# GpSimd and ScalarE make five of the eight parts of the lanes' one-hots

## The reference

```
h = max(layernorm(x), 0)
x = x + attention_layer(h, src, dst, ...)     # weights: softmax over each node's incoming edges
h = max(layernorm(x), 0)
x = x + message_layer(h, [src, dst], etype)   # 4 steps, each: 4 products by edge type,
                                              # segment_sum over the edges, a GRU cell
# attention: segment_sum(exp(e - max) * Wh[src], dst), e from s_s[src] + s_d[dst]
# messages:  etypes = argmax(edge_attr); a = segment_sum(trans[etypes, src], dst)
```

## Time and profile before

| what | value |
|---|---|
| median of three runs | 416.37 us (415.9 to 416.38) |
| the profiled execution | 417.0 us, its span 415.0 us |
| mean granted clock of TensorE | 0.979 of full speed |
| busy over the span: TensorE, VectorE, ScalarE, GpSimd | 88%, 64%, 36%, 24% |

### The profile page before, as it was taken

One profiled execution on the slowest core, in us unless ns is written; L12 is line 12 of the kernel. 1 busy time (PEld: TensorE's weight loads), 2 busy tenths in 40 slices (PEclk: granted clock), 3 DMA queues, 4 the chain that ended last, 5 costly groups with the idle time before them and its releaser, 6 DMA issues.

```text
span 415.0 us, 6625 instructions
## 1 busy us (share of the span) xinstructions
PE 364.1 (88%) x2057; PEld 246.0 (59%) x2057; DVE 265.3 (64%) x797; ACT 150.9 (36%) x333; POOL 99.8 (24%) x139
## 2 busy tenths in 40 slices
PE   1469798778899979887999999999999999999993
PEld 0458455555677756443756755665846566647792
DVE  6899998999998757774456434455444355344134
ACT  3363577444565354432313121323132131213121
POOL 3100300000000001000777002776005773017300
PEclk9969989999999998999999999999999999999998
DMA  5300000000000000123133202242112332012200
GB/s 136 88 1 2 0 2 2 1 2 1 2 2 2 2 0 0 53 101 109 47 105 103 90 0 88 53 146 58 77 44 66 96 114 86 17 76 56 54 14 24
DMA packets 14499, 19.88 MB, mean 48 GB/s; under 512 B 2592, under 2 KB 7729, under 8 KB 14461
## 3 DMA queue, kind: packets, MB, share of 16 engines
q1 hardware_dynamic: 10276, 12.90, 8.8%
q0 software_dynamic: 2912, 5.97, 5.9%
q10 hardware_dynamic: 1272, 0.54, 0.5%
HBM read 8.27 MB, written 11.13 MB: 47 GB/s over the span
## 4 chain that ended last, share of the span: by engine, by line
PE 65%; DVE 21%; issue 6%; ACT 3%; DVEq 2%; POOL 1%; DMA 0%; SPq 0%; ACTq 0%; POOLq 0%
PE small L1635 29%; PE big L1617 8%; DVE cell_hot L977 7%; PE big L1477 4%; PE small L1514 4%; DVE scores L996 3%; DVEq L977 2%; PE small L1656 2%; PE small L1669 2%; PE big L1580 2%; PE big L1582 1%; PE big L1581 1%; PE small L1580 1%; PE small L1571 1%; PE small L1582 1%
## 5 line engine op out<-in xcount | busy, mean ns | idle before, releaser
L1635 PE MATMUL small<-nibbles,store 128*128 128x384 fp8e4 (+1 forms) x640 | 125.8, 353 | 1.7 <-issue 0.9
L482 POOL DMA_INDIRECT scores<-messages,w_gat x91 | 87.0, 956 | 121.5 <-DMA messages<-store 95.0
L1635 PEld LDWEIGHTS small<-nibbles,store 128*128 128x128 f16 x640 | 62.3, 98 | 64.8 <-issue 7.7
L977 DVE TENSOR_SCALAR cell_hot<-iota,cell_w,fields 128x320 bf16<-128x320 f16 x231 | 64.9, 356 | 1.0 <-issue 0.6
L1477 PE MATMUL big<-cell_hot,store 128*128 128x320 bf16 x231 | 43.2, 324 | 13.9 <-DVE cell_hot L977 11.2
L750 ACT CAST store<-digit_words 128x512 f16<-128x512 f32 x40 | 24.6, 618 | 82.6 <-DVE digit_words L1146 82.6
L1146 DVE TENSOR_TENSOR digit_words<-big,edge_rows 128x512 f32<-128x512 f32 x40 | 27.4, 690 | 41.1 <-PE big L1617 41.1
L1477 PEld LDWEIGHTS big<-cell_hot,store 128*128 x231 | 31.3, 144 | 23.3 <-issue 21.1
L1617 PE MATMUL big<-wT,h 128*128 128x512 f32 x80 | 39.8, 615 | 2.3 <-ACT h L746 2.3
L1089 DVE SCALAR_TENSOR_TENSOR cell_hot<-rz,cell_hot 128x256 f32<-128x256 f32 (+2 forms) x29 | 11.0, 380 | 36.3 <-ACT cell_hot L721 36.3
L468 POOL TENSOR_TENSOR rstd<-var_e,power 128x2 f32<-128x2 f32 x5 | 3.5, 696 | 125.7 <-DVE var_e L1134 125.7
(11 more groups left out here) (262 smaller groups left out, 492.2 us busy)
## 6 DMA issues: line engine op xcount, KB each, us to landing
messages<-store SPq DMA_DIRECT2D x40, 256.0 KB, 2.0
scores<-messages,w_gat POOLq DMA_INDIRECT x91, 2.6
xn<-in_x SPq DMA_DIRECT2D x1, 576.0 KB
out<-xn SPq DMA_DIRECT2D x4, 128.0 KB
store<-in_edge_attr SPq DMA_DIRECT2D x1, 256.0 KB
wn<-in_L_gnn_W_edge SPq DMA_DIRECT2D x1, 256.0 KB, 6.6
wn<-in_L_gnn_Wi ACTq DMA_DIRECT2D x1, 192.0 KB, 4.0
wn<-in_L_gnn_Wh_g ACTq DMA_DIRECT2D x1, 192.0 KB, 6.4
```

The costliest lines, as they stand in the source:

```text
L482: g.indirect_dma_start(out=rows16[:, u].rearrange("p a f -> p (a f)"), out_offset=None, in_=table_rows[s % 2][:], in_offset=bass.IndirectO ...
L977: last = v.tensor_scalar(half_hot[:, (before + q) % RING], iota[:, b * HALF:(b + 1) * HALF], cell_w[:, j % CELL_SETS, bass.ds(tile, 1)], f ...
L1635: last = mm(bank[:, 0:w], m16[s % 2][:, i, t, part], A8[:, t % 2, i, lo:lo + w, t // 2], start=(i == 0 and part == 0 and t == 0), stop=(i ...
```

## The change

VectorE makes only parts 0 to 2 (`LANES_DVE`). For parts 3 to 7 three instructions take the place of the comparison: GpSimd subtracts the column's number from the lane into `lane_gap` (`h1` read as 16-bit numbers) and squares the gap in place; ScalarE then makes max(0, 1 - square), which is 1 where the two agree and 0 elsewhere. There is one `lane_gap`, so the gap of a part waits for the bend of the part before it. The windows wait for the bent parts in place of VectorE's.

```diff
+LANES_DVE = 3
...
+        lane_gap = h1[:].bitcast(F16).rearrange("p (l k) -> p l k", l=P)
...
             norm_scale()
 
+            def lane_gaps(k):
+                done = k - LANES_DVE
+                if k == LANES_DVE:
+                    pool.wait_ge(S0.lanes16, 1)
+                    pool.wait_ge(C.lane_no, 1)
+                else:
+                    pool.wait_ge(S0.bent_lanes, done)
+                g.tensor_tensor(lane_gap, lanes16[:, k * LANE_PART:(k + 1) * LANE_PART].unsqueeze(1)
+                                .to_broadcast([P, P, LANE_PART]), lane_no, ALU.subtract).then_inc(S0.lane_gap, 1)
+                pool.wait_ge(S0.lane_gap, done + 1)
+                g.tensor_tensor(lane_gap, lane_gap, lane_gap, ALU.mult).then_inc(S0.lane_square, 1)
+
+            lane_gaps(3)
+            lane_gaps(4)
             pool.wait_ge(S0.bias_sb, 1)
             pool.wait_ge(E1.sq, 1)
...
+            for k in range(5, LANES_MADE[-1]):
+                lane_gaps(k)
+
             def chunk_scale(y, c):
...
+            def lane_bends(k):
+                act.wait_ge(S0.lane_square, k - LANES_DVE + 1)
+                a.activation(lane_hot[:, :, k * LANE_PART:(k + 1) * LANE_PART], lane_gap, ACT.Relu,
+                             bias=ones[:, 0:1], scale=-1.0).then_inc(S0.bent_lanes, 1)
+
...
                 if J == 1:
+                    lane_bends(4)
                     score_row()
+                if J in (3, 4, 5):
+                    lane_bends(J + 2)
                 if there(J - 3):
                     attn_out(J - 3, J - 3)
...
             for j in range(2, CELL_SETS):
                 window_cells(j)
+            lane_bends(3)
             act.wait_ge(S0.Wh_ps, 2)
...
-                for k in range(LANES_MADE[j - 1] if j else 0, LANES_MADE[j]):
+                for k in range(LANES_MADE[j - 1] if j else 0, min(LANES_DVE, LANES_MADE[j])):
                     lane_hots(k)
...
-                pe.wait_ge(S0.lanes, LANES_MADE[j])
+                pe.wait_ge(S0.lanes, min(LANES_DVE, LANES_MADE[j]))
+                if LANES_MADE[j] > LANES_DVE:
+                    pe.wait_ge(S0.bent_lanes, LANES_MADE[j] - LANES_DVE)
```

More of the change, by code:

```diff
@@ L283, in build @@
         C = sems("c_", "limits iota pads const ident ident16 free lane_no")
-        S0 = sems("s0_", "chain lane_rows lanes_T lanes16 rows ranks ranks_T best best_T table fields_T fields b_diag "
+        S0 = sems("s0_", "chain lane_rows lanes_T lanes16 bent_lanes lane_gap lane_square rows ranks ranks_T best best_T table fields_T fields b_diag "
                   "w_T w_sb bias_sb hn stats var rstd norm lanes "
```

## The result

The changed kernel takes 457.5 us (median of four runs, 456.77 to 458.65), the kernel before on the same chip 416.38 us (415.9 to 416.91). The ratio is 1.1002, with a 95% interval of 1.0975 to 1.1028: slower by 41.1 us. The profiled execution has a span of 455.0 us, 40.0 more than before.

The account below looks back on a forecast made before the run. VectorE, working 109.88 of 115 us while edges are counted, was taken to bound the kernel. 10 x 5.5 - 1.1 - 7.0 = +46.9 us gave 463 us, range 416 to 478 (the forecast case alone 431 to 474).

Parts of the forecast that it names:

- VectorE bounds the stretch; the five parts are worth 7.0 us: Edge counting, 20 to 135 us: VectorE works 109.88 of 115 us; five lane parts at 1.40 us leave it.
- 5.5 us per GpSimd instruction: Each gap or square over 128x2560 elements on GpSimd was taken at 5.5 us, between bounds of 2.25 and 6.6.
- The term of 55 us: Ten GpSimd gaps and squares at 5.5 us each, charged to VectorE as standing still.
- The lower reading of the text: GpSimd's gaps and squares: two reads in turn with the write beside them, 4.4 us each.
- A hold of full length: VectorE stands still for the whole of each GpSimd instruction: 463 us; chance 0.72 together with the variant.
- The lenient reading of the power at 17.07 us: GpSimd holds VectorE only while data pass, 2.25 us per instruction: +14.4 us, 431 us, the forecast's own lower end.
- the variant in which VectorE always gets ahead: GpSimd starts only when VectorE runs out of twelve ring slots; 10 us waiting per part, +43 us; chance 0.72 with the forecast.
- The bends at nothing, the waits of TensorE for bent parts at nothing: ScalarE's five bends, 2.4 us each, fit idle time (12 us without cover); TensorE doesn't wait for gap, square and bend, 13.4 us.
- GpSimd's chain for the edge scale: Behind the second gap and square, it ends at 58.6 us, 14 us later, with VectorE arriving 19.5 us later; costs nothing.
- A slow TensorE keeps pace, so new pauses of 5.5 us cost little beyond themselves.: After pauses, at lower clock, TensorE's window products take 0.28 us each, as VectorE's half one-hots do; costed at nothing.
- The 0.66 of the earlier trace: TensorE's mean granted clock in the ten microseconds after its 4.86 us wait, read as partly 1.2 GHz of 2.4.

Follow-up runs that it names:

- e4: Changed kernel with each GpSimd gap and square cut to 20 of 2560 elements, all waits between engines kept: 409.38 us, ratio 0.9829 to the kernel before.
- e1: Kernel before, all eight lane parts on VectorE, plus ten long two-input GpSimd instructions whose results nobody uses: 458.77 us (+42.6).
- e9: Changed kernel with all eight lane parts made by VectorE again and read from there, GpSimd's ten instructions and five bends kept: 460.65 us, ratio 1.1074.
- e6: Changed kernel with the five squares made by ScalarE instead of GpSimd, five GpSimd instructions left: 435.42 us, ratio 1.0462.

## Why the prediction was right

The forecast was 463 us, by a full standing still of VectorE; 457.5 us were measured. Step by step:

- *VectorE bounds the stretch; the five parts are worth 7.0 us.* Right: e4 gives back 6.8 us.
- *5.5 us per GpSimd instruction.* Too long. The gaps last 4.84 us in the mean, the squares 4.45 to 4.58 where they start at once and 5.7 where a lane part is let through first. The term of 55 us measured 49.1 (24.2 + 24.9), and of that VectorE lost 42.9, since the held instruction's own time lies inside the hold. The lower reading of the text, two reads in turn with the write beside them at 4.4 us, was nearer than the one taken.
- *A hold of full length.* Right, and shown by e1 (nobody uses the results) and e4 (the same waits, short instructions). The lenient reading of the power at 17.07 us fell. So did the variant in which VectorE always gets ahead: GpSimd's instruction starts between two of VectorE's, and the next one of VectorE is held.
- *The bends at nothing, the waits of TensorE for bent parts at nothing.* Right for TensorE, which shows no such wait. For the bends e9 leaves at most 3 us in all, of 12 without cover. At the score row VectorE waited for 0.2 us; e6 shows what more work on ScalarE costs there, 2.6 us.
- *GpSimd's chain for the edge scale.* Forecast to end at 58.6 us; its last instruction ended at 57.0 (56.23 and 0.74 us long), and VectorE took the result at 64.86.
- *"A slow TensorE keeps pace, so new pauses of 5.5 us cost little beyond themselves."* This step failed. It was worked out for window products alone, which at the lower clock still match the half one-hots. An aggregate behind a pause takes 4.67 us instead of 2.50, and a VectorE with three parts runs out of ring slots: 3.3 us of waits where there were 0.2. The 0.66 of the earlier trace rows is a mean over 20 to 30 us, of which the first 4 us lie in the wait itself.

The corrected sum is 42.9 - 1.1 - 7.0 + 3.1 = +37.9 us. The waits for counts (1.7 us) and the score row (0.2), which the kernel before doesn't have in this stretch, make it +39.8, for a span that grew by 40.0. The first term was 12.1 us too large, and 5.0 us of waits were missing, so that the sum was 6.9 us above the growth of the span, and the forecast 5.5 us above the median. That it came so near is in part luck: the two errors have opposite signs.

## What to carry to other kernels

An engine with a low busy share is not a free helper. Before work is moved to GpSimd, ask how long each of its instructions keeps VectorE from starting, and charge that to VectorE. A cut of the suspected instruction to a few elements, with all waits left in place, separates the cost of its length from the cost of the hand-overs in one run. And a pause is paid twice where the engine that waited comes back at the lower clock and the engine that paused it has no other work to fill the time.

## What had not been expected of the hardware

- A GpSimd `tensor_scalar` with one input over 128x2560 16-bit elements took 6.73 us, a `tensor_tensor` with two inputs of the same size 4.45 to 4.96 us where it started at once. The Trainium skill, GPSIMD Engine Reference, section "Engine selection", has two-input operations about twice as slow as on VectorE and one-input ones roughly at line rate; the runs here show the one-input form slower than the two-input one. Why, no run here tells.
- Memsets, which only write, took 2.23 us and held half one-hots, but neither the lane parts nor the small operation beside them.
- VectorE doesn't lose every turn between two GpSimd instructions that follow each other at once: at 46.56 us of the changed kernel a lane part gets through, and the square that had started is recorded for 1.28 us longer.
